# Expert results in quarters of batches h and h+4 on 32 by 32 tiles, with the second attention's preparation moved up

## The chip, the cores and the metric

The kernel runs on one core of a Trainium2 chip (trn2). The metric is the device time of one execution in microseconds, as the median of several runs. TensorE is PE in the profile, VectorE is DVE, ScalarE is ACT, GpSimd is POOL, and SyncE, which issues every DMA of this kernel, is SP.

## The reference, cut to what matters

Two blocks follow each other on x of 8 batches, 512 tokens and 512 features, all in float32. Block 0 is cross attention (16 heads, 120 context rows) and then a mixture of experts. Block 1 is cross attention with a mask and biases, and then a feed-forward part with a token shift. The part that this change touches is the mixture's second matrix and the way its result is given back to the tokens in block 1's first lines:

```python
perm = (logits == jnp.max(logits, axis=-3, keepdims=True))          # one token of 32 for each expert (128) and group (128)
permuted = jnp.einsum('bntd,bntes->bnesd', grouped, perm)
inner = jax.nn.relu(jnp.einsum('bnesd,esdf->bnesf', permuted, W1) + b1)
result_permuted = jnp.einsum('bnesf,esdf->bnesd', inner, W2) + b2   # 128 groups x 128 experts x 512
result = jnp.einsum('bnesd,bntes->bntd', result_permuted, perm)
x = x + jnp.tanh(g_ffn[0]) * result
```

There are 128 (expert, set) pairs, called experts here, and 128 groups of 32 tokens, 16 in each batch. `result_permuted` has 128 x 128 rows of 512 floats, 33.5 MB. It doesn't fit on the core, so it goes out to DRAM and is read back batch by batch.

## The kernel before

The program is written out by hand, engine by engine, with semaphores. Its stages run one after the other on each engine: keys and values, attention 0 (`attention` with `lay=0`), `experts`, attention 1 (`lay=1`), `feed_forward`. A stage can hand pieces of its own beginning to the stage ahead of it, so that both interleave.

**Experts.** `experts` gathers the chosen tokens, then `hidden(c, w)` (line 2098) multiplies by W1, 8 steps w for each quarter c of the features. `inner` holds 128 rows, which are 4 experts (a) by 32 hidden units, for each of 32 steps k and 128 groups. After that come 64 steps p of `results(p)`. Step p takes k = p mod 32 and one half h = p // 32 of the groups (64 groups, so batches 0 to 3 or 4 to 7). It has four float32 matmuls (line 2114), one for each a: a weight block of 32 rows by 64 groups (the tile is 32*64), 512 columns. Expert a stands on the rows 32a to 32a+31 of the array and on the column half a mod 2, and two experts share a bank. So each p fills two banks. ACT (line 2010) and DVE (line 2035) copy the banks into one of four slots of 1 MB (`slot(u)`, RO = 4, two of them in `e_chosen` and two in `e_xc`), where u = p // 2. `result_on_act` gives the bank q = 0 to ACT and the bank q = 1 to DVE, and from p = 32 on some q = 1 banks to ACT too. SP then stores the slot with one DMA (line 1963), 32 stores in all. A slot is written again only when the store of four u before has landed. The first 12 steps p interleave with the last `hidden` steps.

**Attention 1.** Each turn i does attention for batch i and prepares batch i+1. Before attention, a batch j needs its experts' rows: 16 loads (`load_experts`, line 703) of 256 KB, four (a) for each tile of 128 tokens (t). Then `merge_tile` (lines 1601, 1602 for the bias, 1606 for the rows), `merged` on DVE (line 1305 and statistics), `variance`, `apply`, `first_norm` (16 transposes, line 1516), three-pass queries (`queries`, lines 157 to 159), scores for the row maxima (`max_tile`, line 1558; DVE reduces them, line 1339) and `max_rows` (line 1567). There is one buffer `a_rp` for the experts' rows, so the rows of batch j+1 are loaded when the merge of batch j is done. From batch 2 on POOL adds a bias into those rows (line 1032).

**What runs between the results.** `behind[0]` calls attention 1's beginning after each results step, so it is batch 0's preparation. On SP (`load_behind`, by u): small loads at u = 7, at u = 16 (`HALF_U`) the wait `half_written` for the first 16 stores, batch 0's 16 loads and the query weight, at 18 the keys, at 22 batch 1's permutation and 16 loads, at 24 x of batch 1, at 28 the values. On PE, ACT and DVE (by p): merge at p = 41, ACT's weights at 43, transposes at 45, queries at 47, 49, 51, 53, maxima at 49 to 56, `max_rows` at 58. After p = 63 come the scores of batch 0 and turn 0. Turn 0's PE order is merge tiles 0 and 1 of batch 1, scores 1, tile 2, values 0, tile 3, scores 2, values 1, scores 3, values 2, `first_norm`, values 3, queries of batch 1. SP begins attention 1's own part by waiting for all 32 stores, and then loads the output weight (line 712).

Of the kernel before, what the change touches and what calls it, by code (L numbers as in the profile page):

```python
# [74 lines left out]
HALF = B // 2  # L75
# [5 lines left out]
MERGE_AT, WEIGHT_AT, NORM_AT, QUERIES_AT, ROWS_AT = 41, 43, 45, (47, 49, 51, 53), 58  # L81
MAXIMA_AT = {49 + n: (n // 2, (0, 1) if n % 2 == 0 else (2, 3)) for n in range(8)}
# [7 lines left out]
Front = namedtuple("Front", "cleared half_written written groups_read spare_banks banks")  # L90
# [463 lines left out]
def attention(nc, lay, io, early, late, sem, eight, after, front=None, turned_place=None):  # L554
# [144 lines left out]
    def load_experts(sp, j, t):  # L699
        of = 0 if isinstance(j, int) and j < HALF else 1  # L700
        src = io["rp"][of].rearrange("u (c j a t) s d -> (u c) s j t a d", c=2, a=GT, t=NT)
        for a in range(GT):
            sp.dma_start(rp[:, t, a:a + 1], src[:, :, bass.ds(j - HALF * of, 1), t, a]).then_inc(rp_in[t], 16)
# [158 lines left out]
    def load_behind(sp, u):  # L862
# [5 lines left out]
        if u == 7:  # L868
# [9 lines left out]
        if u == HALF_U + 2:  # L878
# [14 lines left out]
    HALF_U = EK // 2  # L893
# [614 lines left out]
    def tensor(pe, banks_read=None, step_of=None):  # L1508
# [167 lines left out]
        def turn(i):  # L1676
# [39 lines left out]
            if merging:  # L1716
# [3 lines left out]
            if merging:  # L1720
                merge_tile(i, i + 1, 2)
            values(0)
            if merging:
# [104 lines left out]
def experts(nc, sb, sem, eight, io, behind):  # L1828
# [16 lines left out]
    NH = NG // 2  # L1845
# [45 lines left out]
    def expert(k, a):  # L1891

        q, c = divmod(a, 2)
        return 8 * (k // 2) + 4 * c + 2 * (k % 2) + q

    def result_on_act(p, q):

        return q == 0 or (p >= EK and (p % 2 == 1 or MERGE_AT < p <= NORM_AT))
# [41 lines left out]
    def sync(sp):  # L1940
# [17 lines left out]
        for u in range(EK):  # L1958
# [7 lines left out]
    def half_written(sp):  # L1966
        for q in range(RO):
            sp.wait_ge(out_st[q], 16 * (EK // 2 // RO))
# [116 lines left out]
    def tensor(pe):  # L2085
        def hidden(c, w):
# [6 lines left out]
            for b in range(4):  # L2093
                for a in range(EJ):
                    e = expert(4 * w + b, a) - EW * w
                    rhs = gt[:, w, :, e, :] if turned(c) else gt[:, :, w, e, :]
                    out = hbank[w % 2][a * EF:(a + 1) * EF, b * NG:(b + 1) * NG].rearrange("p (s g) -> p s g", g=GS)
# [4 lines left out]
        def results(p):  # L2102
            k, h = p % EK, p // EK
# [527 lines left out]
```

## Time and profile before

| what | value |
|---|---|
| median of 3 runs | 1330.63 us (1325.4 to 1336.3) |
| the profiled execution's own time | 1328.46 us |
| its span in the trace | 1326.7 us |
| mean granted clock of TensorE | 0.984 of full speed |
| busy: PE, DVE, ACT, POOL | 1258.9, 885.8, 571.2, 554.4 us |
| DRAM read, written | 129.92 MB, 82.62 MB |

The profiled execution took 1328.46 us, which is 1.8 us more than its span (work outside the recorded span) and 2.2 us below the median of the runs. Times in the text such as 607.32 are microseconds from the start of the span. A busy PE counts any matmul in flight, also where only a part of the array works. "GB/s" is what the core's 16 DMA engines moved. "Idle before" in square brackets names what ended the idle time in front of an instruction.

### The profile page before, as it was taken

How to read it: one execution, taken by the hardware profiler on the slowest of the kernel's cores; microseconds unless marked ns; L12 is line 12 of the kernel's file. 1: busy time of each engine (PE TensorE's matmuls, PEld its weight loads, DVE VectorE, ACT ScalarE, POOL GpSimd, SP SyncE). 2: the span in 40 equal slices, each digit the busy share in tenths (PEclk: the TensorE clock that was granted, in tenths of full speed). 3: DMA queues.
4: the chain of work that ended last, by engine and by line, in shares of the span. 5: the costliest groups of instructions: out<-in, count | busy, mean ns of one | idle time of the engine just before them, and what ended most of it. 6: DMA issues, size and time to landing. Idle time of an engine off the chain costs nothing.

```text
span 1326.7 us, 28239 instructions
## 1 busy us (share of the span) xinstructions
PE 1258.9 (95%) x10607; PEld 906.3 (68%) x10607; DVE 885.8 (67%) x1570; ACT 571.2 (43%) x1039; POOL 554.4 (42%) x456
## 2 busy tenths in 40 slices
PE   8999999999999978887989999999998999999998
PEld 7777776777677667621447666766775778888887
DVE  6984787777676546663646766766675977777762
ACT  4345345434542545453562443353336433333331
POOL 3312642454251100000339657856734644444540
PEclk9999999999999979998999999999998999999999
DMA  9765455224411678999983643563323111111101
GB/s 350 225 179 187 154 159 174 101 88 149 141 73 36 208 217 257 321 400 354 400 348 93 222 170 97 174 220 132 121 84 128 64 63 63 63 43 52 63 27 37
DMA packets 126503, 213.59 MB, mean 161 GB/s; under 512 B 27610, under 2 KB 49370, under 8 KB 122332
## 3 DMA queue, kind: packets, MB, share of 16 engines
q1 hardware_dynamic: 126427, 212.57, 47.6%
q8 instruction: 49, 0.80, 0.2%
q14 instruction: 27, 0.21, 0.1%
HBM read 129.92 MB, written 82.62 MB: 160 GB/s over the span
## 4 chain that ended last, share of the span: by engine, by line
PE 77%; DVE 8%; DMA 5%; ACT 4%; issue 3%; SPq 3%; POOL 0%; ACTq 0%; DVEq 0%; POOLq 0%
PE b L157 12%; PE b L158 11%; PE b L159 11%; PE b L1586 5%; PE b L1784 5%; PE b L1785 5%; PE b L1786 5%; PE b L1558 4%; DMA s_rp<-e_chosen 3%; PE b L2080 3%; PE b L1691 3%; PE b L1699 3%; PE b L2098 2%; ACT a_pr L1150 2%; PE b L2114 2%
## 5 line engine op out<-in xcount | busy, mean ns | idle before, releaser
L1150 ACT ACTIVATE a_pr<-b 120x512 f32<-120x512 f32 x252 | 130.2, 603 | 95.1 <-PE b L1586 95.1
L1339 DVE TENSOR_REDUCE a_mx<-b 128x4 f32<-128x480 f32 x256 | 151.9, 651 | 10.4 <-PE b L1558 10.3
L1032 POOL TENSOR_TENSOR a_rp<-a_rp,a_b2s 128x512 f32<-128x512 f32 x96 | 120.5, 1296 | 23.8 <-DMA a_rp<-s_rp 23.8
L1071 POOL TENSOR_TENSOR a_atl<-a_pvs,a_ath 128x512 fp32r<-128x512 f32 x64 | 81.3, 1303 | 81.7 <-ACT a_ath L1194 81.7
L1784 PE MATMUL b<-a_woh,a_ath 128*128 128x512 f32 x256 | 104.6, 409 | 3.1 <-POOL a_atl L1071 3.1
L157 PE MATMUL b<-a_xth,a_wqh 128*128 128x512 f32 x256 | 104.2, 407 | 1.5 <-DVE a_xtl L1314 1.1
L158 PE MATMUL b<-a_xtl,a_wqh 128*128 128x512 f32 x256 | 101.6, 397 | 0.0
L159 PE MATMUL b<-a_xth,a_wql 128*128 128x512 f32 x256 | 101.6, 397 | 0.0
L1786 PE MATMUL b<-a_woh,a_atl 128*128 128x512 f32 x256 | 101.6, 397 | 0.0
L1785 PE MATMUL b<-a_wol,a_ath 128*128 128x512 f32 x256 | 101.5, 397 | 0.0
L1016 POOL TENSOR_TENSOR a_rstd<-a_ve,a_mhalf 128x4 f32<-128x4 f32 x16 | 16.2, 1014 | 190.9 <-DVE a_ve L1261 190.9
L1484 DVE SCALAR_TENSOR_TENSOR a_x<-b,a_gate,a_x 128x512 f32<-128x512 f32 (+1 forms) x64 | 47.8, 747 | 71.8 <-PE b L1786 71.8
L1558 PE MATMUL b<-a_kbd,a_qh 128*128 128x480 f32 x256 | 83.7, 388 | 2.4 <-DMA a_kbd<-s_kh 1.6
L2262 POOL TENSOR_TENSOR f_xmkl<-f_mix,f_xmkh 128x512 fp32r<-128x512 f32 x32 | 48.9, 1541 | 59.9 <-ACT f_xmkh L2274 59.9
L2304 DVE SCALAR_TENSOR_TENSOR f_mix<-f_dif,f_mu,f_xt 128x512 f32<-128x512 f32 x64 | 61.1, 971 | 15.7 <-PE b L159 10.7
L1991 ACT ACTIVATE e_gt<-b 128x512 f32<-128x512 f32 x87 | 46.2, 597 | 49.1 <-PE b L2080 41.1
L1699 PE MATMUL b<-a_pr,a_vals 120*32 120x512 f32 x512 | 66.7, 592 | 0.0
L157 PEld LDWEIGHTS b<-a_xth,a_wqh 128*128 128x128 f32 x256 | 48.4, 189 | 20.9 <-issue 8.7
L834 POOL TENSOR_TENSOR a_xr<-a_xr,a_mr 128x512 f32<-128x512 f32 x28 | 45.7, 1666 | 39.0 <-DMA a_mr<-s_norms 39.0
L1784 PEld LDWEIGHTS b<-a_woh,a_ath 128*128 128x128 f32 x256 | 48.6, 190 | 18.5 <-issue 8.7
L1558 PEld LDWEIGHTS b<-a_kbd,a_qh 128*128 128x128 f32 x256 | 47.1, 188 | 20.3 <-DVE a_mx L1339 5.8
L2114 PE MATMUL b<-e_w,e_inner 32*64 32x512 f32 x384 | 50.2, 622 | 9.1 <-DVE e_chosen L2035 4.5
(245 smaller groups left out, 3142.4 us busy)
## 6 DMA issues: line engine op xcount, KB each, us to landing
a_rp<-s_rp SPq DMA_DIRECT2D x128, 256.0 KB, 4.5
s_x<-a_x SPq DMA_DIRECT2D x16, 1024.0 KB, 4.2
s_rp<-e_chosen SPq DMA_DIRECT2D x16, 1024.0 KB, 8.3
s_rp<-e_xc SPq DMA_DIRECT2D x16, 1024.0 KB, 8.4
e_w<-in_w SPq DMA_DIRECT2D x56, 256.0 KB, 4.8
a_xr<-in_x_t SPq DMA_DIRECT2D x8, 1024.0 KB, 6.6
a_x<-in_x SPq DMA_DIRECT2D x8, 1024.0 KB, 10.7
s_xn<-a_xn SPq DMA_DIRECT2D x8, 1024.0 KB, 4.7
```

Source lines behind the costliest of these rows:

```text
L157: pe.matmul(out, ah, bh, start=(c == 0 and not begun), stop=False)
L158: pe.matmul(out, ah, bl, start=False, stop=False)
L159: last = pe.matmul(out, al, bh, start=False, stop=(c == C - 1))
L1032: pool.tensor_tensor(rp[:, t, a], rp[:, t, a], b2s[:, :], ALU.add).then_inc(rp_biased, 1)
L1071: pool.tensor_tensor(quarter(atl, q), quarter(pvs, q), f(quarter(ath, q)), ALU.subtract).then_inc(a_lo, 1)
L1150: act.activation(pr[:, h % RING, :], bank[k][0:S2, :], ACT.Exp, scale=SCALE)\
L1339: dve.tensor_reduce(mx[:, t, :, r], bank[k][:, 0:HJ * S2].rearrange("p (a s) -> p a s", a=HJ), AX.X, ALU.max).then_inc(free[k], 1)
L1558: pe.matmul(bank[k][:, 0:HJ * S2], qh[:, r, t * P:(t + 1) * P], kbd[:, r, :], start=True, stop=True)\
L1699: ins = pe.matmul(bank["v"][a * DK:(a + 1) * DK, :], v[:, h * DK:(h + 1) * DK], pr[:, h % RING, :], start=True, stop=True)
L1784: pe.matmul(out, ath[:, m, cols], woh[:, m, :], start=(m == 0), stop=False)
L1785: pe.matmul(out, ath[:, m, cols], wol[:, m, :], start=False, stop=False)
L1786: ins = pe.matmul(out, atl[:, m, cols], woh[:, m, :], start=False, stop=(m == C - 1))
```

## The change

- The groups are ordered so that a quarter h holds batches h and h+4 (`hidden` writes and reads in the order `j h g`; only the access patterns differ). `round_of(u)` sets the order of the stores: u = 0 to 7 are quarter 0 for all experts, u = 8 to 31 take quarters 1, 2, 3 in turn for the experts n = 0 to 7.
- `results(p)` has eight matmuls instead of four. Each has a weight block of 32 rows by 32 groups (tile 32*32) and 512 columns. The two row strips a = 2 (p mod 2) + q feed bank q alone, and four steps k = 4n + c fill the four column strips of a bank. So a step p covers four k and half of the rows.
- The experts' rows in DRAM are one tensor of 8 x 128 rows of 18 x 512 floats: four quarters of 8 KB and 4 KB unused. A store is 128 runs of 8 KB at a pitch of 36 KB; before it was 1 MB in one piece. The loads are 128 rows of 2 KB as before.
- Batch 0 is complete after the first 8 stores. Its loads go to u = 9 and wait for 8 stores. Merge, weights, transposes and queries go from p = 41, 43, 45, 47 to 53 to p = 27, 29, 32, 34 to 40; maxima to 36 to 43, `max_rows` to 46.
- Batch 1's permutation and 16 loads go from u = 22 to u = 31 and wait there for all 32 stores. In turn 0 its merge tiles come later: tiles 0 and 1 after scores 2, tiles 2 and 3 after values 1.

```diff
-MERGE_AT, WEIGHT_AT, NORM_AT, QUERIES_AT, ROWS_AT = 41, 43, 45, (47, 49, 51, 53), 58
-MAXIMA_AT = {49 + n: (n // 2, (0, 1) if n % 2 == 0 else (2, 3)) for n in range(8)}
+MERGE_AT, WEIGHT_AT, NORM_AT, QUERIES_AT, ROWS_AT = 27, 29, 32, (34, 36, 38, 40), 46
+MAXIMA_AT = {36 + n: (n // 2, (0, 1) if n % 2 == 0 else (2, 3)) for n in range(8)}
@@ load_experts
-        src = io["rp"][of].rearrange("u (c j a t) s d -> (u c) s j t a d", c=2, a=GT, t=NT)
+        src = io["rp"][:, :, 0:4 * EJ * D].rearrange("u (c j a t) (h s d) -> (u c) s h j t a d", c=4, a=GT, t=NT, s=EJ, d=D)
@@ load_behind
-        if u == 7:
+        if u == 5:
...
-        if u == HALF_U:
-            front.half_written(sp)
+        if u == FRONT_U:                      # EK // 4 + 1 = 9
+            front.front_written(sp)
...
-        if u == 22:
+        if u == EK - 1:
             for k, uses in TW:
                 sp.wait_ge(full[k], uses.n(None, "merge", 1) + 1)
             load_perm(sp, 1)
+            for q in range(4):
+                front.written(sp, q)
             for t in range(NT):
                 load_experts(sp, 1, t)
@@ attention, tensor, turn
+            late = merging and first_turn(i)
-            if merging:
+            if merging and not late:
                 merge_tile(i, i + 1, 0)
                 merge_tile(i, i + 1, 1)
...
             scores(i, i, 2)
+            if late:
+                merge_tile(i, i + 1, 0)
+                merge_tile(i, i + 1, 1)
             values(1)
...
+            if late:
+                merge_tile(i, i + 1, 2)
+                merge_tile(i, i + 1, 3)
@@ experts
+    def round_of(u):
+        if u < EK // 4:
+            return 0, u
+        return 1 + (u - EK // 4) % 3, (u - EK // 4) // 3
-        return q == 0 or (p >= EK and (p % 2 == 1 or MERGE_AT < p <= NORM_AT))
+        return q == 0 or (p >= MERGE_AT and (p % 2 == 1 or MERGE_AT < p <= NORM_AT))
-            sp.dma_start(io["rp"][2 * u // EK][u % (EK // 2)], slot(u)).then_inc(out_st[u % RO], 16)
+            h, n = round_of(u)
+            sp.dma_start(io["rp"][n, :, h * EJ * D:(h + 1) * EJ * D], slot(u).rearrange("p e d -> p (e d)"))\
+              .then_inc(out_st[u % RO], 16)
@@ experts, tensor, results
-            for a in range(EJ):
-                rows, (q, c) = slice(a * EF, (a + 1) * EF), divmod(a, 2)
-                b, _ = result_bank(p, q)
-                ins = pe.matmul(gbank[b][c * NH:(c + 1) * NH, :], inner[rows, k, h * NH:(h + 1) * NH],
-                                w2[k // KS][rows, k % KS, :], start=True, stop=True, skip_group_check=True)
-                if c:
-                    ins.then_inc(g_full[b], 1)
+            for c in range(4):
+                for q in range(2):
+                    a, k = 2 * (p % 2) + q, 4 * n + c
+                    rows, (b, _) = slice(a * EF, (a + 1) * EF), result_bank(p, q)
+                    ins = pe.matmul(gbank[b][c * NQ:(c + 1) * NQ, :], inner[rows, k, h * NQ:(h + 1) * NQ],
+                                    w2[k // KS][rows, k % KS, :], start=True, stop=True, skip_group_check=True)
+                    if c == 3:
+                        ins.then_inc(g_full[b], 1)
@@ build
-    rp_d = [dram(f"s_rp{i}", (EK // 2, P, EJ, D)) for i in range(2)]
+    rp_d = dram("s_rp", (EK // 4, P, 4 * EJ * D + 2 * D))
```

## Rows read from the trace of the kernel before

**Rows 1.** Page, 40 slices of the span: busy tenths of PE and DMA.
```profile
PE   8999999999999978887989999999998999999998
...
DMA  9765455224411678999983643563323111111101
```

**Rows 2.** Windows: stretch, length, busy PE, PEld, DVE, ACT, POOL, clock, DMA share, GB/s.
```profile
557.00:572.00 15.00, 15.00 (x252) 6.98 (x248) 10.47 (x16) 9.06 (x16) 0.00 (x0) 1.00 0.93 365
...
607.00:619.00 12.00, 6.54 (x48) 1.74 (x44) 2.82 (x5) 3.70 (x8) 0.00 (x0) 1.00 0.81 268
619.00:637.00 18.00, 14.36 (x88) 4.60 (x84) 10.39 (x25) 7.82 (x16) 1.41 (x2) 0.81 1.02 384
637.00:668.00 31.00, 29.99 (x164) 14.46 (x164) 17.97 (x30) 13.47 (x25) 12.06 (x19) 1.00 1.03 409
668.00:683.00 15.00, 12.66 (x130) 4.87 (x134) 5.77 (x13) 9.06 (x18) 6.01 (x5) 1.00 0.81 336
```

**Rows 3.** DMA from 557 to 683: GB/s in 40 slices; issues, KB each, us to landing.
```profile
GB/s 341 243 424 403 388 385 416 416 289 419 411 427 427 421 421 419 193 244 280 376 341 392 427 321 426 419 432 390 369 392 402 429 399 428 427 424 424 414 403 39
...
s_rp<-e_chosen SPq DMA_DIRECT2D x16, 1024.0 KB, 8.3
...
a_rp<-s_rp SPq DMA_DIRECT2D x32, 256.0 KB, 6.8
```

**Rows 4.** Timeline of SP's queue: start, length, line, operation, count.
```profile
607.32 11.52 SPq L703 DMA_DIRECT2D a_rp<-s_rp  x16
...
636.55 10.78 SPq L703 DMA_DIRECT2D a_rp<-s_rp  x16
...
671.99 2.67 SPq L1963 DMA_DIRECT2D s_rp<-e_xc  x2
682.80 0.40 SPq L712 DMA_DIRECT2D a_raw_o<-in_o  x1
...
685.86 10.97 SPq L703 DMA_DIRECT2D a_rp<-s_rp  x16
```

**Rows 5.** Timeline of the first and last merge of batch 0, and ACT after it.
```profile
613.66 1.07 PE L1606 MATMUL b<-a_rp,a_permb 128*32 128x512 f32 x8 [1.88 <-DMA a_rp<-s_rp]
...
623.90 1.94 PE L1606 MATMUL b<-a_rp,a_permb 128*32 128x512 f32 x8
...
629.18 2.06 ACT L2010 ACTIVATE e_chosen<-b 128x512 f32<-128x512 f32 x4 [16.95 <-DMA s_rp<-e_chosen]
```

**Rows 6.** Timeline of results steps with no preparation between them.
```profile
571.77 16.59 PE L2114 MATMUL b<-e_w,e_inner 32*64 32x512 f32 x128
...
575.90 0.23 PEld L2114 LDWEIGHTS b<-e_w,e_inner 32*64 32x64 f32 x8 [0.98 <-ACT e_xc L2010]
...
577.11 0.60 ACT L2010 ACTIVATE e_xc<-b 128x512 f32<-128x512 f32 x1 [0.68 <-PE b L2114]
...
577.98 0.23 PEld L2114 LDWEIGHTS b<-e_w,e_inner 32*64 32x64 f32 x8 [0.98 <-issue]
```

**Rows 7.** The matmuls of line 2114: duration of one, ns, min/median/max.
```profile
L2114 PE MATMUL b<-e_w,e_inner x384: 587/587/1111, 568.9 to 672.5; 32*64 32x512 f32 x192
```

**Rows 8.** Timeline of batch 0's queries: first query, two results steps, maxima's rows.
```profile
637.28 0.47 PE L157 MATMUL b<-a_xth,a_wqh 128*128 128x512 f32 x1 [0.78 <-DVE a_xtl L1314]
...
652.14 1.09 PE L2114 MATMUL b<-e_w,e_inner 32*64 32x512 f32 x8
...
658.69 1.09 PE L2114 MATMUL b<-e_w,e_inner 32*64 32x512 f32 x8
...
666.00 0.66 PE L1567 MATMUL b<-a_ident,a_mx 128*128 128x128 f32 x4
```

**Rows 9.** Timeline of turn 0: last merge of batch 1, transposes, POOL's bias.
```profile
684.30 1.07 PE L1606 MATMUL b<-a_rp,a_permb 128*32 128x512 f32 x8
...
691.73 1.97 PE L1516 MATMUL b<-a_ident,a_xn 128*128 128x128 f32 x16
...
693.00 10.00 POOL L1032 TENSOR_TENSOR a_rp<-a_rp,a_b2s 128x512 f32<-128x512 f32 x8 [4.37 <-DMA a_rp<-s_rp]
```

More of the change, by code:

```diff
@@ L699, in load_experts @@
     def load_experts(sp, j, t):
-        of = 0 if isinstance(j, int) and j < HALF else 1
-        src = io["rp"][of].rearrange("u (c j a t) s d -> (u c) s j t a d", c=2, a=GT, t=NT)
+        of = 0 if isinstance(j, int) and j < B // 2 else 1
+        src = io["rp"][:, :, 0:4 * EJ * D].rearrange("u (c j a t) (h s d) -> (u c) s h j t a d", c=4, a=GT, t=NT, s=EJ, d=D)
         for a in range(GT):
-            sp.dma_start(rp[:, t, a:a + 1], src[:, :, bass.ds(j - HALF * of, 1), t, a]).then_inc(rp_in[t], 16)
+            sp.dma_start(rp[:, t, a:a + 1], src[:, :, bass.ds(j - B // 2 * of, 1), of, t, a]).then_inc(rp_in[t], 16)
     def load_perm(sp, j):
@@ L891, in load_behind @@
             load_v(sp, 0)
-    HALF_U = EK // 2
+    FRONT_U = EK // 4 + 1
     def sync(sp):
@@ L1719, in turn @@
             scores(i, i, 1)
-            if merging:
+            if merging and not late:
                 merge_tile(i, i + 1, 2)
             values(0)
-            if merging:
+            if merging and not late:
                 merge_tile(i, i + 1, 3)
@@ L1844, in experts @@
     RB, RO, KS, RW = 6, 4, 8, 4
-    NH = NG // 2
+    NQ = NG // 4
     EARLY = 2
@@ L2094, in hidden @@
                 for a in range(EJ):
-                    e = expert(4 * w + b, a) - EW * w
-                    rhs = gt[:, w, :, e, :] if turned(c) else gt[:, :, w, e, :]
-                    out = hbank[w % 2][a * EF:(a + 1) * EF, b * NG:(b + 1) * NG].rearrange("p (s g) -> p s g", g=GS)
+                    e = EJ * b + a
+                    rhs = (gt[:, w, :, e, :] if turned(c) else gt[:, :, w, e, :]).rearrange("p (j h) g -> p j h g", j=2)
+                    out = hbank[w % 2][a * EF:(a + 1) * EF, b * NG:(b + 1) * NG]\
+                        .rearrange("p (h j g) -> p j h g", j=2, g=GS)
                     ins = pe.matmul(out, w1[:, r % RW, b * EJ + a, :], rhs, start=True, stop=True,
@@ L2102, in results @@
         def results(p):
-            k, h = p % EK, p // EK
-            if k % 4 == 0:
-                pe.wait_ge(relued, k // 4 + 1)
-            if k % KS == 0:
-                pe.wait_ge(w2_in[k // KS], 16 * KS)
-            for q in range(2):
-                b, n = result_bank(p, q)
-                pe.wait_ge(g_free[b], n)
-            for a in range(EJ):
-                rows, (q, c) = slice(a * EF, (a + 1) * EF), divmod(a, 2)
-                b, _ = result_bank(p, q)
-                ins = pe.matmul(gbank[b][c * NH:(c + 1) * NH, :], inner[rows, k, h * NH:(h + 1) * NH],
-                                w2[k // KS][rows, k % KS, :], start=True, stop=True, skip_group_check=True)
-                if c:
-                    ins.then_inc(g_full[b], 1)
+            h, n = round_of(p // 2)
+            if h == 0 and p % 2 == 0:
+                pe.wait_ge(relued, n + 1)
+                if n % 2 == 0:
+                    pe.wait_ge(w2_in[n // 2], 16 * KS)
+            for q in range(2):
+                b, use_of = result_bank(p, q)
+                pe.wait_ge(g_free[b], use_of)
+            for c in range(4):
[6 more added lines that the diff above has]
+                        ins.then_inc(g_full[b], 1)
             behind[0].pe(pe, p)
@@ L2143, in groups_read @@
     def groups_read(pool, number):
-        b, n = result_bank(EK + number * KS - 1, 1)
+        last = max(u for u in range(EK) if round_of(u)[1] < 2 * number)
+        b, n = result_bank(2 * last + 1, 1)
         pool.wait_ge(g_full[b], n + 1)
@@ L2605 @@
     columns = lambda a: a.reshape(C, P).T
-    by_use = lambda a: a.reshape(EK // 2, 2, 2, 2, *a.shape[2:]).transpose(0, 2, 3, 1, *range(4, a.ndim + 2))\
-        .reshape(ES, *a.shape[2:])
+    by_use = lambda a: a.reshape(ES, *a.shape[2:])
     arrays = dict(
```

14 lines of the change are left out of this document (5 added, 9 removed).

## The prediction

> **What bounds the kernel now.** I read the page's slices first, then the windows, the DMA table and the timeline of the results stage. Over the whole span PE is the busy engine; only in slices 15 to 20 is the DMA row at 8 or 9 while PE has a 7 or 8 [rows 1]. The change works in that stage. Its windows show the DMA engines at a share of 0.93 to 1.03 from 557 to 668 us, but for 607 to 619, where batch 0 is fetched [rows 2]. PE has gaps there: 6.5 of 12 us busy, then 14.4 of 18. So the stage is paced mostly by bytes. At full rate the slices show 421 to 428 GB/s [rows 3], and a store of 1.049 MB costs 1.049 / 0.424 = 2.47 us; 32 stores cost 79 us. 16 loads of one batch (4.2 MB) take 10.8 to 11.5 us to issue [rows 4], which at 0.4 MB/us is also about what their bytes need (10.5 us).
>
> One part is not paced by bytes alone. From the first query of batch 0 (637.28) to `max_rows` (666.00) [rows 8], PE is busy 29.99 of 31 us [rows 2]. Two results steps with a query and four maxima between them take 658.69 - 652.14 = 6.55 us, against the 2.47 us of their one store. DMA stays busy there only because batch 1's 16 loads (from 636.55) and x are in the queue [rows 4].
>
> **Anchor points of before.** Batch 0's loads start at 607.32. The last store is issued by 674.7 and all have landed at 682.80, when SP goes on to the output weight [rows 4]. The last merge of batch 1 ends at 684.30 + 1.07 = 685.37 and releases batch 2's loads at 685.86; the transposes start at 691.73, and POOL's bias at 693.00 [rows 4, 9]. Everything after that is the same work in both kernels, so the change is worth what it does to these last four times.
>
> **The change, part by part.**
>
> 1. *Batch 0's loads earlier.* They wait for 8 stores instead of 16: 8 x 2.47 = 19.8 us less, 607.3 - 19.8 = 587.5. The small loads at u = 5 instead of 7 are ahead in both cases. The last merge of batch 0 starts 16.6 us after the first load (623.90 - 607.32), the slot that ACT waits for lands after 21.9 us (629.18 - 607.32) [rows 4, 5], because SP issues 16 loads before the next store. Both distances are kept, so ACT goes on at 587.5 + 21.9 = 609.4.
>
> 2. *Preparation of batch 0.* Before, the first query comes 8.1 us after that point with five results steps (42 to 46); now there are six (28 to 33), one more at 1.1 us [rows 8]: 618.6. From first query to `max_rows` before: 28.7 us for 11 steps; now 12 steps, 29.8 us: 648.4. In this stretch DMA has the stores only: about six for 30 us. It goes idle for some 12 us, since batch 1's loads no longer fill it.
>
> 3. *The rest of the stores.* 17 results steps are left (p = 47 to 63). Engines need 577.98 - 575.90 = 2.08 us for two steps [rows 6], so 17.7 us; DMA needs 9 stores at 2.47 plus x (2.5) and values (0.6), 25.3 us. DMA sets the end: 650 + 25.3 + about 1.5 for the last landing = 676.8. That is 6.0 us sooner than 682.80.
>
> 4. *Batch 1's loads last.* They now start only then. The nearest rows are the 16 loads elsewhere: issue takes 10.8 to 11.5 us. The last one lands some 3 to 6.8 us after its issue (6.8 is the median with a full queue [rows 3], half of it is my estimate for an empty one), so the last merge ends about 15.5 us after the start: 676.8 + 0.4 + 15.5 = 692.7, against 685.37: +7.3 us. PE's scores 1 and 2 and values 0 lie in this wait but do not fill it. After the last merge less PE work is left in front of the transposes, so DVE's chain sets them; before they came 6.4 us after the merge with PE in use all the while, now I take 5.5. Transposes: +6.4 us. POOL's bias follows batch 2's loads: before 7.1 us behind their issue, of which some 3 us are the output weight's bytes ahead of them in the queue. That weight is now behind batch 1's loads as well, so +7 there, less a little. I take +6.5 for both.
>
> 5. *Eight matmuls of 32*32 for four of 32*64.* Before, 8 records (two for each float32 matmul) take 1.09 us [rows 8] at 587 ns each [rows 7]. Four streams of two passes one after another would take 4 x 2 x 0.43 us; so the four tiles run side by side and the step is two passes long, 2 x 0.43 + 0.2. In 32*32 form the step has 16 records. If all eight tiles run side by side, it costs the issue of eight more weight loads at (0.23 - 0.13) / 7 = 15 ns [rows 6], 0.1 us. If the array takes them in fours, the step is two rounds of two passes less one overlapped, 0.43 us longer. The lower bound is a gain: neighbouring steps now use different row strips and can overlap, 0.43 us for a pair, where no bank is awaited. The round of fill and copy at 2.08 us for two steps [rows 6] hides that gain, and the 2.47 us of a store hides the round. The 14 steps among full-array matmuls (28 to 46, less pairs) are not hidden: +1 us with eight side by side, +6 us in fours. I take +1: four column strips already run side by side in the merge (8 records in 1.07 us [rows 5]) and four row strips in the results.
>
>  The Trainium skill (TensorEngine Tiling (Array Packing), Restrictions and Gotchas) says that different row tiles cannot access the same PSUM bank at once. By that, the old form would pay two rounds for its two experts in a bank, and the new form, with one row strip for each bank, would save 0.86 us in each step. The trace does not agree: 8 records in 1.09 us leave no room for it [rows 8]. Were it so all the same, the gain would stand behind the stores as the 0.43 us do, and would count only in the second of the rivals below.
>
> 6. *Layout.* Stores keep their size. Runs of 8 KB at a pitch of 36 KB are not in this trace; the loads of 2 KB rows are the worst nearby, and in their window the rate over the share is 268 / 0.81 = 331 GB/s [rows 2], against 424: at most +0.7 us a store. I take 0, since 8 KB runs are longer.
>
>  [...]
>
> 7. *Other edits.* `hidden`'s new access patterns cost nothing that the 0.93 share would not hide. POOL's tables are due at p = 63 and move up; they have slack. PE waits in turn 0 for the loads, and the clock fell to half for part of 619 to 637 after such a wait (0.81) [rows 2]: 0 to 3 us, I take 1.
>
> **Sum.** +6.5 + 1 + 1 = +8.5, less 2 for the dip of 607 to 619 (268 GB/s), which shrinks because two stores instead of one lie in the queue when the loads begin: +6.5 us. On the profiled 1328.46 that is 1335; on the median 1330.6 it is 1337.
>
> **The rivals.**
>
> - *Bytes only (not slower).* If the engines keep up in the preparation, all bytes up to batch 1's merge are the same and only their order differs. The end is then 682.80 minus the idle DMA time of before (two slices around 607 at half rate, 3 us, and part of the start), plus 1 us for the wait between the last store and the first load, and the same 2.6 us to the merge: -3 us, 1328. It decides if DMA idles less than 5 us between 617 and 648. For it: the DMA shares of before. Against it: 6.55 us for a store in that stretch.
> - *Engines, not bytes, pace the stage (faster).* If a busy DMA share only mirrors full queues, tiles side by side save 0.43 us in each of 64 steps, 27 us, of which the late loads take back 11: 1315. For it: PE at 29.99 of 31 us. Against it: 2.08 us for two steps is a wait for the copies, not for PE.
> - *Tiles in fours (slower).* +6 us more among the preparation, and two steps then take 2.5 us, at par with a store: 1344. For it: the before kernel never has more than four tiles in a round.
> - *Slower stores.* At 331 GB/s, 32 x 0.7 = 22 us, less 6 idle: 1353.
> - *The late loads cost nothing*, hidden behind turn 0. It would take loads that end before PE runs out of other work: scores 1, values 0 and scores 2 are some 8 us of the 17 between the last store's issue and the transposes [rows 4, 9], and the loads end some 22 us after it. I give this no chance of its own.
>
> **Numbers.** My forecast (1332 to 1341) 0.43; bytes only 0.19; fours 0.20; slower stores 0.09; engines pace it 0.09. One per cent, 13 us, is about what a measurement of this kernel can tell from no change. Slower by over that: half of fours, the slower stores and a tail of the forecast, 0.23. Faster: 0.08. Same: 0.69. The range reaches from bytes only to a little above fours: 1325 to 1349.
>
> **What would show it.** Line 703's first loads at 585 to 590; `max_rows` at 645 to 652; a DMA share under 0.7 in the queries' stretch; all stores landed at 673 to 680; line 1606's last record of batch 1 at 689 to 694; 16 records of line 2114 in 1.1 to 1.3 us. If these come in 1.5 us, it is fours; if stores land at less than 400 GB/s in the tail, it is the layout. I am wrong in the main if DMA stays full through the queries.

## The result, and the profile after

The changed kernel takes 1347.6 us (median of 4 runs, 1345.13 to 1350.18); the kernel before, on the same chip, 1331.31. The ratio is 1.0125 with a 95% interval of 1.0099 to 1.0152: slower by 16.3 us. That lies inside the predicted range of 1325 to 1349 us, but 10.6 us above the forecast of 1337, outside its own span of 1332 to 1341, and past the 1% within which I had given it 0.69.

The profiled execution took 1350.18 us, 2.6 above the median of its kernel, where that of before was below it; the two profiles are 21.7 us apart, the medians 16.3. From its page (busy tenths of PE, tenths of the granted clock, busy tenths of DMA; 33.7 us a slice):

```profile
span 1348.4 us, 29260 instructions
...
PE   9999999999999988888878999999998999999998
...
PEclk9999999999999979957969999999999999999999
DMA  9885456324420688999786534653433211111101
```

Two things are new against [rows 1]: the clock row falls to 5 and 6 in the results stage, and the DMA row, which stood at 8 or 9 in all of it, has a 7 in the slice from 640 to 674 us (the 6 two slices on lies behind the stage). The windows by stage (columns as in [rows 2]) from the first results matmul (563.63, before 557.1) to the issue of the output weight:

```profile
563.60:578.60 15.00, 12.25 (x319) 5.92 (x318) 9.71 (x15) 8.32 (x16) 0.00 (x0) 1.00 0.89 346
578.60:613.00 34.40, 29.58 (x321) 6.04 (x313) 14.19 (x24) 12.01 (x22) 2.83 (x5) 0.50 0.95 339
613.00:631.30 18.30, 14.00 (x152) 5.57 (x148) 11.75 (x27) 9.45 (x18) 1.02 (x1) 0.72 1.01 400
631.30:659.50 28.20, 27.63 (x265) 13.70 (x257) 16.64 (x27) 13.62 (x24) 10.48 (x16) 1.00 0.56 229
659.50:685.00 25.50, 19.93 (x279) 4.24 (x276) 6.28 (x10) 13.95 (x26) 1.97 (x3) 0.66 0.99 379
685.00:693.60 8.60, 4.81 (x52) 2.87 (x48) 0.34 (x1) 3.56 (x7) 5.95 (x5) 0.50 0.76 307
693.60:704.10 10.50, 6.62 (x72) 2.96 (x68) 1.44 (x3) 4.32 (x9) 0.00 (x0) 0.94 0.82 269
563.60:704.10 140.50, 114.82 (x1420) 41.30 (x1420) 60.35 (x105) 65.23 (x121) 22.25 (x30) 0.74 0.86 326
```

The fourth row is the queries' stretch, batch 0's first query to `max_rows`. TensorE is as busy as before, but the DMA share is 0.56 and not 1.03 [rows 2]: 0.44 x 28.2 = 12.4 us of idle time, counted as if all 16 DMA engines stood still together. The granted clock was 0.50, the lower of its two levels (1.2 GHz), for 34 us at the start of the results and for much of 659 to 694, where TensorE waits for copies and slots between two packed steps; before, no stretch of [rows 2] had less than 0.81 (inside the one with 0.81, the 7 us from 618 had 0.58). Those are the two suspects. SyncE's timeline gives the anchor points (DMA issues; answers to [rows 4]):

```profile
595.85 1.92 SPq L702 DMA_DIRECT2D a_rp<-s_rp  x2
...
686.53 0.33 SPq L1973 DMA_DIRECT2D s_rp<-e_xc  x1
686.96 0.55 SPq L705 DMA_DIRECT2D a_permb<-s_perm  x1
693.64 10.25 SPq L702 DMA_DIRECT2D a_rp<-s_rp  x16
704.06 0.48 SPq L711 DMA_DIRECT2D a_raw_o<-in_o  x1
```

Batch 1's loads go out at 693.64, when every store has landed. And the end of the stage, in the timeline of all engines (answers to [rows 9]):

```profile
709.91 1.06 PE L1607 MATMUL b<-a_rp,a_permb 128*32 128x512 f32 x8 [1.52 <-DMA a_rp<-s_rp]
...
716.36 1.97 PE L1517 MATMUL b<-a_ident,a_xn 128*128 128x128 f32 x16 [2.39 <-DVE a_xn L1296]
...
718.70 1.29 POOL L1033 TENSOR_TENSOR a_rp<-a_rp,a_b2s 128x512 f32<-128x512 f32 x1 [4.44 <-DMA a_rp<-s_rp]
```

The transposes start at 716.36, 24.6 us later than before. Of these, 6.5 us are there when the results begin, and 4.5 of them already at the first matmul of `hidden` (494.7, before 490.2). The new access patterns in `hidden` show no cost: one of its matmuls has the same median, 273 ns, and the same extremes, 269 and 422 ns, in both kernels, and from its first to the first results matmul it is 68.9 us against 66.9, in runs of the old patterns 66.9 to 72.7. The start of the results lies anywhere from 555.9 to 566.4 in the profiled executions of all kernels below, so I count from the first results matmul from here on. By that count, in us:

| | before | forecast | after |
|---|---|---|---|
| batch 0's loads start | 50.2 | 30.4 | 32.2 |
| ACT goes on | 72.1 | 52.3 | 55.9 |
| first query | 80.2 | 61.5 | 67.7 |
| `max_rows` | 108.9 | 91.3 | 95.8 |
| all stores landed | 125.7 | 119.7 | 130.0 |
| last merge of batch 1 ends | 128.3 | 135.6 | 147.3 |
| transposes | 134.6 | 141.0 | 152.7 |

Up to `max_rows` the order is as forecast, with delays of up to 6.2 us. Between `max_rows` and the last landing another 6 us are lost: 34.2 us instead of 28.4. Behind it the forecast's distances hold within 2 us.

### The profile page after: what moved, and what is told of

Same layout as the page of the kernel before. It is cut to its first block, busy times and chain, and to the rows that moved or that the text cites. A ratio compares the mean times of both kernels' runs of the same rounds, so it can differ in the third digit from the quotient of the medians.

```text
span 1348.4 us, 29260 instructions
## 1 busy us (share of the span) xinstructions
PE 1267.6 (94%) x11119; PEld 907.5 (67%) x11119; DVE 884.3 (66%) x1566; ACT 572.5 (42%) x1043; POOL 552.8 (41%) x456
## 4 chain that ended last, share of the span: by engine, by line
PE 73%; DVE 8%; DMA 6%; ACT 3%; issue 3%; POOL 3%; SPq 3%; DVEq 0%; ACTq 0%; POOLq 0%
PE b L156 12%; PE b L157 11%; PE b L158 11%; PE b L1587 5%; PE b L1792 4%; PE b L1559 4%; PE b L1793 4%; PE b L1794 4%; PE b L2091 3%; PE b L2127 3%; PE b L1692 3%; PE b L1700 2%; PE b L2110 2%; ACT a_pr L1151 2%; SPq L702 2%
## 5 line engine op out<-in xcount | busy, mean ns | idle before, releaser
L1340 DVE TENSOR_REDUCE a_mx<-b 128x4 f32<-128x480 f32 x256 | 152.0, 649 | 13.6 <-PE b L1559 13.4
L1033 POOL TENSOR_TENSOR a_rp<-a_rp,a_b2s 128x512 f32<-128x512 f32 x96 | 120.4, 1292 | 25.7 <-DMA a_rp<-s_rp 25.7
L1485 DVE SCALAR_TENSOR_TENSOR a_x<-b,a_gate,a_x 128x512 f32<-128x512 f32 (+1 forms) x64 | 47.7, 746 | 72.7 <-PE b L1794 72.7
L2318 DVE SCALAR_TENSOR_TENSOR f_mix<-f_dif,f_mu,f_xt 128x512 f32<-128x512 f32 x64 | 63.0, 1001 | 14.7 <-PE b L158 10.7
L2127 PE MATMUL b<-e_w,e_inner 32*32 32x512 f32 x768 | 50.0, 786 | 11.8 <-ACT e_xc L2021 6.7
```

Of the source, the lines that this page charges most:

```text
L1033: pool.tensor_tensor(rp[:, t, a], rp[:, t, a], b2s[:, :], ALU.add).then_inc(rp_biased, 1)
L1340: dve.tensor_reduce(mx[:, t, :, r], bank[k][:, 0:HJ * S2].rearrange("p (a s) -> p a s", a=HJ), AX.X, ALU.max).then_inc(free[k], 1)
L2127: ins = pe.matmul(gbank[b][c * NQ:(c + 1) * NQ, :], inner[rows, k, h * NQ:(h + 1) * NQ], w2[k // KS][rows, k % KS, :], start=True, stop=Tr ...
```

## Experiments

All kernels compute everything. The filler matmuls of some write into a PSUM bank that nobody reads at that point. I had two causes in mind: **late loads** (batch 1's fetch exposed behind the last store) and **half clock** (packed tiles leave TensorE with gaps). A third way of looking at it, a ledger of busy and idle DMA time, came only from the runs themselves.

**1. The tiles alone.** The kernel before, each 32*64 matmul split in two:

```
-            for a in range(EJ):
+            for half in range(2):
+                for a in range(EJ):
...
+                    to, of = c * NH + half * NH // 2, h * NH + half * NH // 2
+                    ins = pe.matmul(gbank[b][to:to + NH // 2, :], inner[rows, k, of:of + NH // 2],
```

> The kernel before, with each 32x64 matmul of the results split into two of 32x32 (eight for a step p instead of four, 256 matmuls more). Schedule, layout in DRAM and loads are those of before. Theory A (the new form costs nothing by itself; it is the gaps it leaves on PE that let the clock fall): a step still keeps each of its tiles busy for two passes and the next step uses the same tiles, so no gaps are added; the same within 3 us of before, half clock for no more than 15 us between 557 and 683. Rival B (the form itself costs, by twice the instructions or by tiles taken in fours): 0.43 us for a step among full-array matmuls or more waits for instructions, 6 us slower or more.

Measured: 1331.88 us, ratio 1.0016 (0.9993 to 1.0039). Sixteen records instead of eight cost nothing that can be told from noise (the interval reaches to 5.2 us), and the rival with tiles in fours falls: it asked for 6 us or more. The changed kernel's own timeline shows it too, at full clock:

```profile
563.63 1.22 PE L2127 MATMUL b<-e_xc,e_inner 32*32 32x512 f32 x32
...
658.42 1.09 PE L2127 MATMUL b<-e_w,e_inner 32*32 32x512 f32 x16 [0.56 <-DVE e_xc L2046]
...
662.44 1.49 PE L2127 MATMUL b<-e_w,e_inner 32*32 32x512 f32 x32 [0.81 <-ACT e_xc L2021]
664.84 1.49 PE L2127 MATMUL b<-e_w,e_inner 32*32 32x512 f32 x32 [0.91 <-ACT e_chosen L2021]
667.23 2.36 PE L2127 MATMUL b<-e_w,e_inner 32*32 32x512 f32 x32 [0.91 <-ACT e_chosen L2021]
670.25 2.36 PE L2127 MATMUL b<-e_w,e_inner 32*32 32x512 f32 x32 [0.66 <-ACT e_xc L2021]
```

One step alone takes 1.09 us, as before [rows 8]; two neighbouring steps overlap and take 1.22 to 1.49 us. In the kernel before, two took

```profile
557.11 1.95 PE L2114 MATMUL b<-e_xc,e_inner 32*64 32x512 f32 x16
```

and in experiment 1 just the same:

```profile
561.82 1.95 PE L2116 MATMUL b<-e_xc,e_inner 32*32 32x512 f32 x32
```

There each step still uses all four row strips for both column halves, so the next step finds none free. So the overlap comes with the changed kernel's assignment of row strips, not with the smaller tiles alone. In the first listing, the last two rows are at half clock: 2.36 us, and a round of 3.0 us instead of 2.4.

**2. Late loads alone.** The kernel before, with the changed kernel's wait and its later merges in turn 0:

```
-        if u == 22:
+        if u == EK - 1:
...
+            for q in range(4):
+                front.written(sp, q)
```

> The kernel before (32x64 tiles, halves, preparation at its old steps) with batch 1's permutation and 16 loads moved from u = 22 to u = 31 behind the wait for all stores, and its merge tiles in turn 0 after scores 2 and values 1 as in the kernel after. Nothing else. Theory A (step 4 of the prediction: the loads are exposed for some 13 us, and the stage in front of them gets shorter by only 3 to 5 us, because the stretch of the queries is paced by the engines): 8 to 10 us slower than before, 1340. Rival B (bytes pace everything): the stage gets shorter by the loads' 10.8 us, so 2 to 3 us slower, 1334.

Measured: 1342.68 us, ratio 1.0095 (1.006 to 1.0129), +13.5 us, without packing and without quarters: more than either theory had (8 to 10 and 2 to 3 us). So this edit by itself makes a loss nearly as large as the whole change. The last store is issued 117.4 us behind the first results matmul, against 117.2 in the kernel before: taking 4.2 MB of loads out from between the stores has not brought the last of them forward at all. This speaks against the forecast's step 3. The queries' stretch and the whole stage show why:

```profile
641.50:670.20 28.70, 28.29 (x157) 13.82 (x153) 15.95 (x26) 11.93 (x21) 12.45 (x19) 1.00 0.69 270
560.40:695.20 134.80, 110.37 (x908) 42.76 (x908) 63.90 (x109) 64.25 (x117) 22.25 (x30) 0.92 0.89 339
```

TensorE needs its 28.7 us for that stretch in either case. Before, the 16 loads filled it with bytes; here it idles at 0.69.

**3. The clock restored.** The changed kernel, with one matmul that nobody needs behind each pair of steps outside the preparation:

```
+            if p % 2 and (15 <= p < MERGE_AT - 1 or p > ROWS_AT):
+                pe.matmul(eight[7][:, :], inner[:, 0, :], inner[:, 0:4, :].rearrange("p k n -> p (k n)"),
```

> The kernel after, with one float32 matmul of 128x128 by 512 columns, whose result nobody reads, behind every odd results step from 15 to 25 and from 47 to 63 (15 matmuls, some 13 us of PE time added). Theory A (PE's gaps between packed steps are what lets the clock fall to half, 34 us from 578.8 and 27 us from 667.5 in the profile of after, and this makes the stage longer): the clock stays up, two steps take some 2.4 us instead of 2.98, and the kernel is 4 to 8 us faster than after, near 1341. Rival B (the low clock is hidden behind the stores): 0 to 8 us slower than after, since work was added.

Measured: 1345.82 us, ratio 1.0121 (1.0091 to 1.0152), clock 0.978. The clock is mostly back (0.85 from 578 to 613 and 0.97 from 654 to 685), the time hardly: far from theory A's 1341, at the lower end of rival B's 0 to 8 us slower. A filler of that length fills the round itself (two steps and filler 2.56 us), so I ran one of half the length:

```
+                pe.matmul(eight[7][:, 0:256], inner[:, 0, :], inner[:, 0:2, :].rearrange("p k n -> p (k n)"),
```

> The changed kernel with filler matmuls half as long (256 columns) at the places of the first filler run. There the filler brought the granted clock back but filled TensorE's round itself: two packed steps of 1.43 us and the filler's 1.13 make 2.56 us, as long as two steps at half clock. In the changed kernel two steps at full clock come every 2.40 us (660.03, 662.44, 664.84, 667.23) and at half clock every 3.0 to 3.3. Theory A (half clock and late loads are the causes): if the short filler holds the clock, the last landing comes 5 to 8 us sooner than in the changed kernel, measured from the first results matmul, and the time is 1340 to 1344, the late loads' 11 to 13 us remaining. If it does not hold the clock: 1345 to 1349. Rival D (the clock is a bystander and the last quarter is set by the stores): clock held, but landing still at 125 us or later behind the first results matmul, 1345 or more.

Measured: 1348.35 us, ratio 1.0126 (1.0096 to 1.0156). In the tail, where the clock now holds up to 680 (from there to the last landing it is 0.63, in the changed kernel 0.50):

```profile
660.00:680.00 20.00, 17.77 (x250) 5.24 (x242) 4.84 (x7) 12.16 (x22) 1.96 (x3) 0.99 0.97 368
```

The granted clock is 0.99 and the DMA share 0.97. In the changed kernel the same 20 us have a clock of 0.69 and the same share and rate (0.97, 367 GB/s). All stores have landed 127.3 us behind the first results matmul instead of 130.0. That is rival D's forecast: in the tail the clock is a bystander. From `max_rows` to the last landing it is 33.4 us here and 33.5 with the long fillers (clock 0.95 throughout), against 34.2 without any. Up to the first query the profiles do show a difference, 65.7 and 63.0 us against 67.7, which the medians don't. The control, the same fillers (full length) in the kernel before:

> Control: the kernel before with the same filler matmuls (13 up to the preparation, 3 behind it). If a filler is hidden behind waits of TensorE, 1328 to 1333 and clock 0.98 as before. If it costs its full length of some 1.7 us anywhere TensorE is not waiting, up to +20 us; then the filler runs understate what the clock is worth by that.

Measured: 1332.42 us, ratio 1.002 (0.9997 to 1.0044). The fillers cost 5.9 us at most by the interval, 1.9 by the medians, and so hide nothing large.

**4. Batch 1's loads inside.** The changed kernel with batch 1's quarter stored by u = 19 and its loads at u = 21, its merges in turn 0 where the kernel before has them, and `max_rows` at p = 52:

```
+        if u < 14:
+            return 1 + (u - EK // 4) % 3, (u - EK // 4) // 3
+        if u < 20:
+            return 1, u - 12
+        return 2 + (u - 20) % 2, 2 + (u - 20) // 2
...
-        if u == EK - 1:
+        if u == 21:
```

> The kernel after with another order of stores from u = 14 on: quarter 1 is finished at u = 19 (n = 2 to 7), quarters 2 and 3 follow in turn. Batch 1's permutation and loads go to u = 21 behind the wait for 20 stores, its merge tiles in turn 0 are where they are in the kernel before, and max_rows is at p = 52 instead of 46 (its target is read by the weights of n = 4 until p = 51). Tiles, layout and the rest are those of after. Theory A (the late loads cost about half of what was lost, by their exposure of 17 us and by the idle DMA in the queries' stretch): 8 to 11 us faster than after, 1338. Rival B (the loss is the clock's, with packed tiles): within 3 us of after, 1346. Were both to hold in part, the difference says how much.

Measured: 1347.49 us, ratio 1.0123 (1.0088 to 1.0158). The loads are no longer late, and nothing is gained. With the fillers as well:

> The kernel with batch 1's loads inside the results (1347.5) plus the filler matmuls that brought the granted clock from 0.961 to 0.978 in the changed kernel. Theory A (the late loads and the half clock are the two causes, each hidden behind the other when only one is removed): with both gone, near the kernel before, 1327 to 1334, the transposes of batch 0 in the second attention within 137 us of the first results matmul (before 134.6, changed 152.8, late loads alone 147.1). Rival B (the stage with batch 1's loads inside is held up by something else, such as DMA share or waits of the preparation): 1342 to 1346, transposes still at 145 or later. In between, 1335 to 1341: both, in proportion.

Measured: 1341.82 us, ratio 1.0086 (1.0052 to 1.012). Its median is lower than without them, though the intervals meet, and the stage in question has not become shorter (136.9 us in its profile, 136.7 without). It is still 11 us slower than the kernel before, and the transposes come 145.8 us behind the first results matmul, as rival B had it. So late loads and half clock were not the whole story. The run without fillers shows what both share with the changed kernel:

```profile
627.80:662.30 34.50, 33.41 (x357) 14.89 (x353) 18.75 (x30) 18.13 (x33) 4.46 (x8) 1.00 0.65 250
562.80:699.50 136.70, 112.41 (x1352) 38.07 (x1352) 60.55 (x105) 60.87 (x112) 22.22 (x30) 0.75 0.89 344
```

The queries' stretch has come forward, and the loads are issued behind most of it: the DMA share is 0.65 in 34.5 us, 12 us idle, as in the changed kernel.

**5. The layout.** The changed kernel, each store one contiguous 1 MB:

```
-            sp.dma_start(io["rp"][n, :, h * EJ * D:(h + 1) * EJ * D], slot(u).rearrange("p e d -> p (e d)"))\
+            sp.dma_start(io["rp"][h, n], slot(u).rearrange("p e d -> p (e d)"))\
...
-    rp_d = dram("s_rp", (EK // 4, P, 4 * EJ * D + 2 * D))
+    rp_d = dram("s_rp", (4, EK // 4, P, EJ * D))
```

> The changed kernel with each store one contiguous 1 MB (the four quarters in four blocks of the scratch) instead of 128 runs of 8 KB at a pitch of 36 KB; nothing else differs. Theory A (the layout costs nothing): 1345 to 1350, stage as long as in the changed kernel. Rival C (scattered stores are slower: 361 GB/s at a share of 0.99 in the changed kernel's second 20 us of the stage, against 399 at 1.02 before): 0.2 to 0.25 us for each of 32 stores, 1339 to 1343, with 395 GB/s or more in that window.

Measured: 1345.91 us, ratio 1.0103 (1.0059 to 1.0148); the interval holds the changed kernel's 1.0125. Batch 1's loads take 10.27 us to issue, there 10.25. The rate in the window in question (583.6 to 603.6 us) is 359 GB/s, as low as the 361 with scattered stores, so the layout of the stores doesn't make it low. The same holds for the tail (663.6 to 683.6): 379 GB/s in both kernels. The rival with slower stores falls.

**6. Sooner preparation.** The changed kernel with fillers and late loads, but batch 0's loads at u = 16, the small loads at u = 7 and the preparation back at 41 to 58:

```
-MERGE_AT, WEIGHT_AT, NORM_AT, QUERIES_AT, ROWS_AT = 27, 29, 32, (34, 36, 38, 40), 46
+MERGE_AT, WEIGHT_AT, NORM_AT, QUERIES_AT, ROWS_AT = 41, 43, 45, (47, 49, 51, 53), 58
...
-        if u == FRONT_U:
+        if u == EK // 2:
```

> The changed kernel with filler matmuls (1345.8) and batch 0's loads and preparation back where the kernel before has them (loads behind 16 of the results' issues instead of 9, merge at 41, rows at 58). It tells what 'preparation sooner' is worth by itself with the late loads kept. Forecast step 3 (it brings the last landing forward by 6 us): 1350 to 1354. Theory A (the late loads cost 13 and the sooner preparation gives back next to nothing): 1343 to 1348. If the sooner preparation harms: 1338 to 1342.

Measured: 1342.58 us (1333.83 to 1346.68), ratio 1.01 (1.0066 to 1.0135), against 1.0121 with the sooner preparation. The intervals meet. The sooner preparation gives back nothing that shows; whether it costs some us is open.

**7. Quarters in the old order.** Now the reverse: tiles, quarters and layout of the changed kernel, batch 0's loads behind its eight stores, but preparation and batch 1's loads where the kernel before has them:

```
+        if u < EK // 2:
+            return 1, u - EK // 4
+        return 2 + (u - EK // 2) % 2, (u - EK // 2) // 2
...
-        if u == EK - 1:
+        if u == 22:
```

> Quarters, the new layout and the packed tiles as in the changed kernel, batch 0's loads behind its eight stores, but the preparation at the results steps of the kernel before (merge 41, rows 58), batch 1's quarter stored second, its loads at u = 22 inside the queries' stretch and its merges where the kernel before has them. Of the change only tiles, layout and batch 0's sooner loads are left. Theory A: no late loads, and the queries' stretch is filled with bytes again; what remains is the half clock of packed tiles, some 3 to 6 us: 1331 to 1337, transposes 134 to 140 us behind the first results matmul. Rival E (quarters or layout cost by themselves): 1340 or more.

> The run with quarters in the old order, plus the short filler matmuls. Theory A (both causes gone, and TensorE no longer waits for batch 0's loads at the merge, which landed long before): 1324 to 1331, at or a little below the kernel before. If the filler costs or does not hold the clock: as without it, 1331 to 1337. Rival E: 1340 or more.

Measured: 1341.92 us, ratio 1.0091 (1.0063 to 1.0119), and with the short fillers 1339.37 us, ratio 1.0062 (1.0041 to 1.0083). I had expected 1331 to 1337 and 1324 to 1331: both misses. The first fits the number of rival E (quarters or layout cost, 1340 or more), the second just misses it; experiment 8 decides on that rival. The windows of the first:

```profile
590.00:640.00 50.00, 31.78 (x328) 6.96 (x328) 17.38 (x31) 12.31 (x23) 0.00 (x0) 0.56 0.98 376
640.00:660.00 20.00, 17.94 (x208) 9.89 (x204) 13.60 (x30) 13.26 (x25) 9.01 (x14) 0.91 0.72 262
560.20:692.50 132.30, 102.07 (x1353) 37.66 (x1356) 64.79 (x114) 55.54 (x103) 22.23 (x30) 0.81 0.92 354
```

From 590 to 640 the DMA engines are full although TensorE works only 31.8 of 50 us: batch 0's loads came in a stretch that had bytes enough without them. At 640 to 660, when TensorE turns to the preparation and stores come slowly, those loads are spent and batch 1's are not out before 648.71: 0.28 x 20 = 5.6 us idle.

**The account.** These rows led me to add it up for all kernels: the time from the first results matmul to the issue of the output weight, and the DMA share in it. The kernel before:

```profile
637.30:666.00 28.70, 28.30 (x153) 13.79 (x153) 17.17 (x28) 12.42 (x22) 11.91 (x18) 1.00 1.03 407
557.10:682.80 125.70, 107.87 (x898) 40.50 (x898) 65.94 (x113) 61.48 (x112) 22.31 (x30) 0.96 0.96 377
```

Length times share is the stage's busy DMA time, the rest is idle. The last column is the median against that of the kernel before on the same chip; us throughout:

| kernel | length | share | busy | idle | time against before |
|---|---|---|---|---|---|
| before | 125.7 | 0.96 | 120.7 | 5.0 | |
| tiles alone | 125.4 | 0.96 | 120.4 | 5.0 | +2.7 |
| before, fillers | 124.2 | 0.96 | 119.2 | 5.0 | +1.9 |
| quarters, old order, fillers | 130.8 | 0.93 | 121.6 | 9.2 | +8.7 |
| quarters, old order | 132.3 | 0.92 | 121.7 | 10.6 | +11.3 |
| changed, old positions, fillers | 133.8 | 0.90 | 120.4 | 13.4 | +12.0 |
| late loads alone | 134.8 | 0.89 | 120.0 | 14.8 | +13.5 |
| batch 1 inside | 136.7 | 0.89 | 121.7 | 15.0 | +18.3 |
| batch 1 inside, fillers | 136.9 | 0.89 | 121.8 | 15.1 | +11.3 |
| changed, fillers | 135.4 | 0.87 | 117.8 | 17.6 | +16.6 |
| changed, whole stores | 136.9 | 0.87 | 119.1 | 17.8 | +15.4 |
| changed, half fillers | 138.2 | 0.86 | 118.9 | 19.3 | +17.7 |
| changed | 140.5 | 0.86 | 120.8 | 19.7 | +16.3 |

The busy time is 118 to 122 us in every kernel. What differs is the idle rest, and the time goes with it, if roughly: it stands 1.2 to 5.7 us above what the idle time adds, and 8.3 us for "batch 1 inside".

Three cautions. Length and share come from one profiled execution of each kernel, the last column from medians; the profile of "changed, old positions, fillers" took 1333.83 us, 8.8 us less than its median. The share has two decimals, so an idle time is good to 0.7 us. And a constant busy time follows from nearly the same bytes (45.4 to 47.4 MB in the stage) whatever paces them: the ledger tells where the time lies, and only an edit can tell why. The last run was that edit.

**8. The order of the kernel before, with everything else changed.** As in experiment 7, with batch 0's loads at u = 16 too:

```
-        if u == FRONT_U:
+        if u == EK // 2:
```

> Quarters, packed 32x32 tiles and the new layout, with batch 0's loads at u = 16, batch 1's at u = 22 and all of the preparation where the kernel before has them. So far, from the first results matmul to the issue of the output weight, length times DMA share is 118 to 122 us in every kernel (before 125.7 x 0.96 = 120.7, changed 140.5 x 0.86 = 120.8, late loads alone 134.8 x 0.89, sooner loads of batch 0 alone 132.3 x 0.92); what differs is the idle rest: 5.0, 19.7, 14.8 and 10.6 us. Theory F (bytes set the stage, and only idle time of the DMA engines makes a kernel longer): the idle rest is 4 to 7 us here too, the stage 124 to 127 us and the time 1328 to 1334, whatever TensorE's clock does. Rival B (half clock of packed tiles costs by itself): clock about 0.97 and 1334 to 1338. Rival E (quarters or layout cost): 1338 or more.

Measured: 1332.68 us, ratio 1.0027 (1.0002 to 1.0051). The two stretches up to batch 0's merge, and the whole stage:

```profile
560.00:588.00 28.00, 22.20 (x516) 8.55 (x512) 17.40 (x27) 14.71 (x28) 2.83 (x5) 1.00 0.89 346
588.00:623.00 35.00, 34.28 (x336) 6.74 (x340) 16.05 (x27) 13.66 (x24) 0.00 (x0) 0.51 1.01 393
560.00:683.55 123.55, 108.12 (x1352) 37.93 (x1352) 65.29 (x114) 56.44 (x103) 22.24 (x30) 0.81 0.98 382
```

Here is the half clock of the changed kernel, 35 us at 0.51, and under it a DMA share of 1.01: no DMA time is lost to it. The stage is 123.55 us long, busy 121.1, idle 2.5, no longer than in the kernel before. The time is as theory F had it; stage and idle time came out just under its ranges. Yet the kernel is not faster by the 2.5 us that idle time fell but slower by 2.6, so the ledger misses 5 us here. By the interval, quarters, tiles, layout and half clock together cost 0.3 to 6.8 us, and rival E's 1338 or more is out, though single runs reach 1338.44.

The changed kernel's loss thus lies mainly in where the loads and the preparation stand, and its two parts don't add: late loads alone cost 13.5 us, batch 0's sooner loads alone (with tiles and layout) 11.3, both together 16.3. No version that I ran is faster than the kernel before; by the ledger it had only 5 us of idle DMA time to give.

## Why the prediction was right or wrong

**Steps 1 and 2 (batch 0 sooner, idle in the queries' stretch): right.** The first loads start at 32.2 us, forecast 30.4. The DMA share in the queries' stretch is 0.56, forecast under 0.7, and the idle time 12.4 us, forecast "some 12". The first query is 6.2 us late by that count, since ACT goes on 3.6 us late and the six steps behind it run partly at half clock (0.72 in 613 to 631). The clock's part in these 6.2 us isn't settled: with fillers the profiles had 2.0 and 4.7 us less, the medians nothing.

**Step 3 (all stores landed 6.0 us sooner): this is the step that failed.** By the common count the landing came 4.3 us later than before and 10.3 later than forecast. 4.5 us of these were there at `max_rows`. The rest is a mis-sized term: I counted 9 stores, x and values behind `max_rows`. The DMA table from 659.5 to 694 has

```profile
DMA packets 2294, 12.32 MB, mean 357 GB/s; under 512 B 223, under 2 KB 223, under 8 KB 983
```

so 12.3 MB, and not 9 x 1.049 + 1.05 + 0.24 = 10.7: a store of before is still in flight, and `perm` comes too. The sum also starts at 650, 1.6 us behind its own `max_rows`. The mean rate up to 693.6 is 361 GB/s where I took 424 throughout, with a share of 0.99 up to 685 and 0.76 behind it. Bytes set this tail, as I had written, not the clock: with the clock restored it is 0.7 to 0.8 us shorter (experiment 3). I had also written that stores landing at less than 400 GB/s in the tail would mean the layout. They did (379 at a share of 0.99), and so they did with whole stores (experiment 5): that sign was a wrong one.

Above all the sum contradicted its own parts. [Rows 2] and [rows 3] say that bytes pace this stage. Then an edit that moves no byte can only change the stage by the idle time that it makes or removes. Step 2 found 12 us of new idle time, yet step 3 went on to a landing 6 us sooner and step 4 to a stage only some 6 us longer, with a new wait for the last landing on top. Before: 5.0 us idle. With the forecast's own numbers, in hindsight: these 5.0, less 2 for the dip at batch 0's loads, 12 in the queries' stretch and 2 for the last landing (1.5) and the step to the first load (0.4) make 17, or +12 for the stage. Measured: 19.7, +14.8. That one line of accounting, with the +2 for tiles and clock, would have given about 1345.

**Step 4 (the loads last, +7.3 for the last merge): the distances were right, the anchor wrong.** From first load to last merge 17.3 us against my 15.5; from there to the transposes 5.4 us against 5.5. From transposes to the end nothing is new: the output weight is issued 644.3 us before the end of the span, 643.9 in the kernel before.

**Step 5 (tiles, +1): right in kind.** Eight side by side: 16 records in 1.09 us. The gain for a pair was larger than my 0.43 us (1.95 us for two steps before, now 1.22 to 1.49), and it hid behind the stores as forecast. What I did not foresee is that faster steps leave TensorE with gaps in which its clock is halved.

**Step 7 (clock, +1): if the number is right, it is by luck.** 0.50 for 34 us and again in the tail is far more than a dip. But experiment 8 shows 35 us of it under a full DMA queue, with no idle time there. With fillers the ratio differs by -0.0004 (changed), +0.0001 (changed, half as long), -0.0037 (batch 1 inside) and -0.0029 (old order), each with intervals that meet: 0 to 5 us. The stage in the profiles was 135.4 us (changed, fillers) and 138.2 (half as long) against 140.5. How much of the changed kernel's loss the clock makes stays open within these 5 us. `hidden`'s access patterns, put at nothing in the same step, show no cost.

**Step 6 (layout, 0): right,** by experiment 5. Batch 1's late loads take 10.23 us to issue at the old pitch of 512 KiB between 8 KB pieces (experiment 2), 10.25 in the changed kernel (1152 KiB) and 10.27 with whole stores (256 KiB).

**The rivals.** "Bytes only" had the right mechanism and the right test (it decides if DMA idles less than 5 us in the queries' stretch); it idled 12.4. "Engines pace the stage" forecast 27 us of gain from faster steps. The steps did become faster (two take 1.22 to 1.49 us instead of 1.95), yet with the old order around them the kernel gained nothing: experiment 8 refutes this rival, as experiment 1 does "fours" and experiment 5 "slower stores". I had no rival in which the idle time simply adds. That 1347.6 lies in the range at all is luck: its upper end stood for tiles in fours, and they did not come.

**What stays open.** The times stand 1.2 to 5.7 us above what the idle time adds, in the unchanged tiles too (fillers in the kernel before: +1.9 at equal idle time), and 8.3 us for "batch 1 inside" without fillers. Part of it is how the profiled executions lie: that of before was 2.2 us under its median, and outside the stage the profiles differ by up to 10.5 us in its start and 5 us behind its end. What the rest is, no run shows.

## What to carry to other kernels

Where the DMA share is near one, keep a ledger: busy DMA time was nearly fixed by the bytes (118 to 122 us here), and an edit that only reorders them cost about what idle time it opened, wherever that lay. Bulk loads are worth most where a compute-bound stretch would leave the queues empty; bringing them "sooner", into a stretch that is full anyway, or "last", behind everything, both take them from there. Speed of an engine off that path, and its clock, then count for little: 0 to 5 us here. Test the ledger with an edit, since the constant busy time alone proves nothing.

## What the runs showed of the hardware that I had not expected

- With packed steps that overlap, TensorE's granted clock stayed at half for long. With 32*64 tiles the lowest mean clock of a stretch of the results was 0.81 in 18 us [rows 2]; with 32*32 tiles that overlap it was 0.50 in 34.4 us, while TensorE did two steps and then waited some 0.4 to 0.9 us for a copy. One unneeded matmul of 256 columns behind each pair kept it at 0.99 from 660 to 680. 32*32 tiles without the overlap (experiment 1) had the same mean clock as before, 0.984.
- In the old form two row strips wrote into one PSUM bank, on different partitions, without taking turns: a step of 8 records takes 1.09 us, no longer than one of 16 records in the new form, where one row strip feeds each bank.
- Neighbouring packed steps on different row strips can overlap almost wholly: 32 records in 1.22 us, 16 in 1.09.
